# The output stage of a low-rank mixing kernel, by pairs of tiles with seven products

## The chip, the cores and the metric

One core of a Trainium2 chip. The metric is device time in microseconds. A kernel's number is the median of its runs.

## The reference

`x` is 32 sequences of 64 tokens with 1024 features; each sequence has one id of 0 to 7. Cut to what matters:

```python
base   = x @ W.T
logits = x @ Wr.T + 5.0 * one_hot(id)            # 8 experts
gates  = softmax over the two largest logits, 0 elsewhere
h      = einsum('btd,erd->bter', x, A)           # rank 16 for each expert
c      = base + 2.0 * einsum('bter,bte,eor->bto', h, gates, B)
out    = x + c @ (U * S @ V.T).T                 # rank 256
```

The kernel never forms `c`. It computes P = W^T V (1024 x 256) and (B^T V), then for each tile of 128 tokens z = x P + (gated h) (2 B^T V), 128 x 256, and the output z (U S)^T + x.

## The kernel before

All is float32 accuracy made of two reduced parts: each operand is split into `hi` (a cast to fp32r, on ACT) and `lo` (the difference, on DVE or POOL), and `triple` (L243) makes three matmuls of it: hi hi, hi lo, lo hi. There are 16 tiles and five queues that run on their own, held together by semaphores.

- **Start.** W and V arrive in chunks; TensorE makes P in two halves of 8 chunks (`p_chunk`), with ACT and DVE splitting each chunk (`split_w`, `split_v`) in the order i = 0 to 15. P's banks are split into `proj_hi`, `proj_lo`.
- **TensorE, `step(s)`.** `project(s, k)` for 8 values of k (24 matmuls of 392 columns: 128 for h, 8 logits, 256 for z); within it `transpose_gh(s-1)` after k = 1 and `mix(s-1)` after k = 4, which adds the gated part into tile s-1's z; then `transpose_z(s-1)` and the output of tile s-2, `expand(s-2, n)` for two halves of 512 columns, 6 matmuls of 128x512 each. Four banks `fin` are used in turn. Step 2 differs: gh at k = 5, mixing after the last k.
- **DVE, `step(s)`.** `split_gh(s-1)`, `gates_top(s)` (begins at L509 when tile s is projected), `gates_apply(s)` (waits for ACT's exponential), then `residual(s-2, 0)`, `split_z(s-1)`, `residual(s-2, 1)`: bank plus x, into `x_all`.
- **ACT, `step(s)`.** `split_x(s+1)` (xT_hi, L428), the copies `ghT_hi` (L439), `z_sb` (L441), `zT_hi` (L443), then the exponential of tile s (L446). Each waits for its input in that order.
- **POOL.** Only xT_lo (L237) for tiles 0 to 15. TensorE's step s waits for xT_lo of tile s; ACT's xT_hi of tile t waits until tile t-2 is projected.
- **SP.** All loads and stores; the ids (8 KB) after W, then the second tile, S and U. DVE converts them (L593) and compares them (L595) after `b_lo` (L590) and before the gates of tile 0. `us_hi`, `us_lo` (L431, L502) are U times S, of 128x1024 each for m = 0, 1.

After step 15 TensorE still has the outputs of tiles 13, 14 and 15 (36 matmuls' worth of 128x512), with the gh and z of tile 15 between.

## Time and profile before

| | us |
|---|---|
| median of 3 runs (163.03 to 164.63) | 163.12 |
| profiled execution | 163.83 |
| its span, first to last instruction | 161.8 |
| TensorE busy | 156.5 |
| DVE busy | 83.8 |
| ACT busy | 55.4 |
| POOL busy | 40.4 |

Times within the execution are counted from the start of its span. A row of the timeline gives an instruction's start and duration; matmuls overlap, so the engine's pace is read from start to start, not from the duration. What an instruction waited for stands behind it in brackets. The granted clock of TensorE is 1.00 throughout.

### The profile page before, as it was taken

Reading aid. Unit: us, or ns where it says so; the run is one execution under the profiler, and the core shown is the slowest. Engines: PE = TensorE matmul, PEld = TensorE weight load, DVE = VectorE, ACT = ScalarE, POOL = GpSimd, SP = SyncE. Lnnn points to the kernel's source line nnn. Section 1 sums busy time; section 2 is a strip of 40 time slices with the busy share of each in tenths; the row PEclk is TensorE's granted clock in tenths of the full one; section 3 lists DMA queues with packets and bytes.
Section 4 is the critical chain, followed back from the end, with each engine's and each line's share of the span. In section 5 each row is a group of like instructions: output and inputs, shape, how many; then the busy total and the mean of one; then the engine's idle time right before and its main releaser. Section 6 shows DMA issues by size and latency. Waiting matters only on the chain.

```text
span 161.8 us, 2469 instructions
## 1 busy us (share of the span) xinstructions
PE 156.5 (97%) x900; PEld 144.9 (90%) x900; DVE 83.8 (52%) x260; ACT 55.4 (34%) x132; POOL 40.4 (25%) x31
## 2 busy tenths in 40 slices
PE   7899999999899999999999999999999999999992
PEld 4899999999798989898999999898989898989882
DVE  0785785298855271727263535445362627180843
ACT  4765783317334142313223141404141313111210
POOL 2000041070552450505050505050514233200000
DMA  5999999963030659293929393847463430303055
GB/s 176 406 409 400 388 412 408 409 250 130 14 120 0 195 197 297 93 315 110 321 99 302 120 293 124 271 136 253 147 242 134 130 130 0 130 4 130 0 198 191
DMA packets 10522, 32.69 MB, mean 202 GB/s; under 512 B 1424, under 2 KB 1936, under 8 KB 10384
## 3 DMA queue, kind: packets, MB, share of 16 engines
q1 hardware_dynamic: 10224, 31.96, 55.1%
q10 hardware_dynamic: 288, 0.59, 1.0%
q8 instruction: 7, 0.11, 0.3%
q14 instruction: 3, 0.02, 0.0%
HBM read 24.16 MB, written 8.39 MB: 201 GB/s over the span
## 4 chain that ended last, share of the span: by engine, by line
PE 87%; DVE 4%; ACT 3%; DMA 3%; issue 1%; SPq 0%; DVEq 0%
PE fin L244 14%; PE pj L244 14%; PE fin L246 14%; PE fin L245 14%; PE pj L246 14%; PE pj L245 14%; DMA vw_raw<-in_VW 3%; PE zt L303 2%; DVE ids_f L593 1%; PE gt L291 1%; ACT us_hi L431 1%; DVE proj_lo L496 1%; DVE b_lo L590 1%; ACT xT_hi L428 1%; DVE w_lo L487 0%
## 5 line engine op out<-in xcount | busy, mean ns | idle before, releaser
L237 POOL TENSOR_TENSOR xT_lo<-xt_raw,xT_hi 128x1024 fp32r<-128x1024 f32 x16 | 39.3, 2455 | 97.4 <-ACT xT_hi L428 97.4
L244 PE MATMUL pj<-proj_hi,xT_hi 128*128 128x392 f32 x128 | 45.0, 352 | 0.0
L246 PE MATMUL pj<-proj_hi,xT_lo 128*128 128x392 f32 x128 | 43.6, 341 | 0.0
L245 PE MATMUL pj<-proj_lo,xT_hi 128*128 128x392 f32 x128 | 43.4, 339 | 0.0
L244 PE MATMUL fin<-us_hi,zT_hi 128*128 128x512 f32 (+1 forms) x66 | 27.0, 409 | 0.0
L245 PE MATMUL fin<-us_lo,zT_hi 128*128 128x512 f32 (+1 forms) x66 | 25.6, 388 | 0.0
L246 PE MATMUL fin<-us_hi,zT_lo 128*128 128x512 f32 (+1 forms) x66 | 25.6, 388 | 0.0
L244 PEld LDWEIGHTS pj<-proj_hi,xT_hi 128*128 128x128 f32 x128 | 24.0, 188 | 1.1
L245 PEld LDWEIGHTS pj<-proj_lo,xT_hi 128*128 128x128 f32 x128 | 24.1, 188 | 0.6
L246 PEld LDWEIGHTS pj<-proj_hi,xT_lo 128*128 128x128 f32 x128 | 24.0, 188 | 0.0
L509 DVE SCALAR_TENSOR_TENSOR logit<-target,pj 128x8 f32<-128x8 f32 x16 | 2.6, 163 | 39.3 <-PE pj L246 39.3
L554 DVE TENSOR_TENSOR x_all<-fin,x_all 128x512 f32<-128x512 f32 x31 | 21.2, 686 | 2.5 <-PE fin L246 2.5
L244 PE MATMUL fin<-v_hi,w_hi 128*128 128x256 f32 x60 | 17.8, 297 | 0.1
L245 PE MATMUL fin<-v_lo,w_hi 128*128 128x256 f32 x60 | 17.6, 293 | 0.0
L246 PE MATMUL fin<-v_hi,w_lo 128*128 128x256 f32 x60 | 17.5, 292 | 0.0
L428 ACT CAST xT_hi<-xt_raw 128x1024 fp32r<-128x1024 f32 x16 | 16.6, 1039 | 0.0
L246 PEld LDWEIGHTS fin<-us_hi,zT_lo 128*128 128x128 f32 x66 | 12.4, 188 | 2.8
L441 ACT COPY z_sb<-pj 128x256 f32<-128x256 f32 x16 | 6.0, 372 | 25.8 <-PE pj L246 25.8
L439 ACT CAST ghT_hi<-gt 128x128 fp32r<-128x128 f32 x16 | 4.2, 265 | 30.3 <-PE gt L291 30.3
L244 PEld LDWEIGHTS fin<-us_hi,zT_hi 128*128 128x128 f32 x66 | 12.4, 188 | 2.1
L245 PEld LDWEIGHTS fin<-us_lo,zT_hi 128*128 128x128 f32 x66 | 12.5, 189 | 2.0
L443 ACT CAST zT_hi<-zt 128x256 fp32r<-128x256 f32 x16 | 6.0, 374 | 22.2 <-PE zt L303 22.2
(71 smaller groups left out, 195.2 us busy)
## 6 DMA issues: line engine op xcount, KB each, us to landing
xt_raw<-in_xt SPq DMA_DIRECT2D x16, 512.0 KB, 4.2
x_all<-in_x SPq DMA_DIRECT2D x16, 512.0 KB, 3.8
out<-x_all SPq DMA_DIRECT2D x14, 512.0 KB, 2.9
vw_raw<-in_VW SPq DMA_DIRECT2D x6, 384.0 KB, 6.2
w_raw<-in_W SPq DMA_DIRECT2D x8, 256.0 KB, 9.9
u_raw<-in_U SPq DMA_DIRECT2D x1, 1024.0 KB, 12.6
out<-x_all SPq DMA_DIRECT2D x3, 256.0 KB, 2.0
aw_raw<-in_AW SPq DMA_DIRECT2D x1, 544.0 KB, 8.3
```

The costliest lines, as they stand in the source:

```text
L237: nc.gpsimd.tensor_sub(xT_lo[:, t % 2, :, :], xt_raw[:, t % XTR, :, :], xT_hi[:, t % 2, :, :].bitcast(F32)).then_inc(xt_lo, 1)
L244: nc.tensor.matmul(dst, l_hi, r_hi, start=first, stop=False, skip_group_check=shared)
L245: nc.tensor.matmul(dst, l_hi, r_lo, start=False, stop=False, skip_group_check=shared)
L246: return nc.tensor.matmul(dst, l_lo, r_hi, start=False, stop=last, skip_group_check=shared)
L291: nc.tensor.transpose(gt[:, 0:P], gh[:, :], ident[:, :]).then_inc(gt_done, 1)
L303: last = nc.tensor.transpose(zt[:, m * P:(m + 1) * P], z_sb[:, m * P:(m + 1) * P], ident[:, :])
L428: nc.scalar.copy(xT_hi[:, t % 2, :, :], xt_raw[:, t % XTR, :, :]).then_inc(xt_hi, 1)
L439: nc.scalar.copy(ghT_hi[:, :], gt[:, 0:P]).then_inc(gt_hi, 1)
L441: nc.scalar.copy(z_sb[:, :], pj[(s - 1) % 2][:, Z0:COLS]).then_inc(z_copied, 1)
L443: nc.scalar.copy(zT_hi[:, (s - 1) % 2, :], zt[:, 0:RANK]).then_inc(zt_hi, 1)
L509: nc.vector.scalar_tensor_tensor(logit[:, :], target[:, s, :], LANG_BIAS, pj[q][:, LOG:LOG + E], ALU.mult, ALU.add).then_inc(gate_step, 1)
L554: nc.vector.tensor_add(x_all[:, t % XR, cols], fin_bank(i)[:, :], x_all[:, t % XR, cols]).then_inc(fin_free, 1)
```

## The change

The output of two tiles (128 rows each) by two halves of U S (m = 0, 1) and two column halves is a 2 x 2 block product. It is done in Strassen's form (Winograd's variant) with 7 products instead of 8, each a `triple` of 128x512. Sums on the z side (`sums`, four of 128 columns, DVE) and on the U S side (`make_tsum`, four of 128x512, POOL, once) go before, and sums of products after: `copy_u` (ACT), `up` (DVE), `side` (POOL, adds into x_all), and four residuals. Each sum is split into hi and lo anew (`split_zb`, `split_t`). Pairs 0 to 6 go that way, in two parts: five products after an odd step, two after the even step behind it. Tiles 14 and 15 are done plainly as before. A pair's outputs begin after step 2p+3, so after step 15 there are 45 matmuls' worth of 128x512. In step 2 and 3 gh stands at k = 4 and mixing after k = 6. z of an odd tile goes to the other half of bank `zt`. The ids are loaded before W and converted in `make_target` at i = 8 of DVE's splitting order. The core of the diff:

```diff
+            def store_pair(p):
+                sp.wait_ge(fin_read, READS * p + 6)
+                sp.dma_start(out_v[2 * p, :, :], x_all[:, (2 * p) % XR, :]).then_inc(stored[(2 * p) % XR], 16)
+                sp.wait_ge(side_add, ADDS * p + 3)
+                sp.dma_start(out_v[2 * p + 1, :, :], x_all[:, (2 * p + 1) % XR, :]).then_inc(stored[(2 * p + 1) % XR], 16)
...
             load_w(0)
             load_w(1)
             sp.dma_start(aw_raw[:, :, :], AW).then_inc(aw_load, 16)
@@ -195,7 +223,6 @@
...
-            for t in range(TILES):
+
+            def split_x(t):
                 pool.wait_ge(xt_hi, t + 1)
                 nc.gpsimd.tensor_sub(xT_lo[:, t % 2, :, :], xt_raw[:, t % XTR, :, :],
                                      xT_hi[:, t % 2, :, :].bitcast(F32)).then_inc(xt_lo, 1)
+
+            def make_tsum():
+                pool.wait_ge(y_done, 2)
+                nc.gpsimd.tensor_sub(tsum[:, 0, :], y[:, 0, BANK:], y[:, 0, 0:BANK]).then_inc(tsum_done, 1)
+                nc.gpsimd.tensor_sub(tsum[:, 2, :], y[:, 1, BANK:], y[:, 0, BANK:]).then_inc(tsum_done, 1)
+                pool.wait_ge(tsum_done, 1)
+                nc.gpsimd.tensor_sub(tsum[:, 1, :], y[:, 1, BANK:], tsum[:, 0, :]).then_inc(tsum_done, 1)
+                pool.wait_ge(tsum_done, 3)
+                nc.gpsimd.tensor_sub(tsum[:, 3, :], y[:, 1, 0:BANK], tsum[:, 1, :]).then_inc(tsum_done, 1)
+
+            def side(t, n, j):
+                cols = slice(n * BANK, (n + 1) * BANK)
+                pool.wait_ge(x_load[t % XR], 16 * (t // XR + 1))
+                nc.gpsimd.tensor_add(x_all[:, t % XR, cols], x_all[:, t % XR, cols], ups[:, j, :]).then_inc(side_add, 1)
+
+            for t in range(3):
+                split_x(t)
+            make_tsum()
+            split_x(3)
+            split_x(4)
+            for p in range(SP_PAIRS):
+                pool.wait_ge(fin_read, READS * p + 1)
+                side(2 * p + 1, 0, 1)
+                side(2 * p, 1, 1)
+                if 2 * p + 5 < TILES:
+                    split_x(2 * p + 5)
+                pool.wait_ge(fin_read, READS * p + 3)
+                side(2 * p + 1, 1, 2)
+                if 2 * p + 6 < TILES:
+                    split_x(2 * p + 6)
 
 
         @block.tensor
...
             def transpose_z(t):
                 pe.wait_ge(z_copied, t + 1)
-                if t >= 1:
-                    pe.wait_ge(zt_lo, t)
+                if t >= 2 and t % 2 == 0:
+                    pe.wait_ge(za_lo, t // 2)
+                    pe.wait_ge(sums_done, 4 * (t // 2))
+                if t >= 2 and t % 2 == 1:
+                    pe.wait_ge(sums_done, 4 * (t // 2))
+                c = RANK * (t % 2)
                 for m in range(MC):
...
+            def product(p, dst, x, y_hi, y_lo, first, last):
+                q = p % 2
+                triple(dst[:, :], zh[:, q, x, :], zl[:, q, x, :], y_hi, y_lo, first, last, shared=True).then_inc(prod, 1)
+
...
+            def p1(p):
+                pe.wait_ge(za_lo, p + 1)
+                if p >= 1:
+                    pe.wait_ge(fin_read, READS * (p - 1) + 4)
+                product(p, bank_a, 0, *us(0, 0), True, False)
+
+            def p6(p):
+                pe.wait_ge(zb_lo, p + 1)
+                if p >= 1:
+                    pe.wait_ge(fin_read, READS * (p - 1) + 1)
+                product(p, bank_b, 4, *t_of(1), True, True)
+
+            def p7(p):
+                if p >= 1:
+                    pe.wait_ge(fin_read, READS * (p - 1) + 5)
+                product(p, bank_c, 5, *t_of(2), True, False)
+
+            def p5(p):
+                if p >= 1:
+                    pe.wait_ge(fin_read, READS * (p - 1) + 6)
+                product(p, bank_d, 3, *t_of(0), True, False)
+
...
+            def p2(p):
+                pe.wait_ge(u_copied, p + 1)
+                product(p, bank_a, 1, *us(1, 0), False, True)
+
+            def p4(p):
+                pe.wait_ge(fin_read, READS * p + 2)
+                product(p, bank_c, 2, *t_of(3), False, True)
+
+            def p3(p):
+                pe.wait_ge(fin_read, READS * p + 3)
+                product(p, bank_d, 6, *us(1, 1), False, True)
+
+            def first_part(p):
+                if p == 0:
+                    pe.wait_ge(us_lo_done, MC)
+                    pe.wait_ge(tl_done, 2)
+                p1(p)
+                p6(p)
+                p7(p)
+                p5(p)
+                p2(p)
+
+            def second_part(p):
+                p4(p)
+                p3(p)
+
+            def expand_end(dst, x, lo, hi):
+                q = (PAIRS - 1) % 2
                 for m in range(MC):
-                    zk = slice(m * P, (m + 1) * P)
-                    last = triple(fin_bank(i)[:, 0:BANK // 2], zT_hi[:, q, zk], zT_lo[:, q, zk],
-                                  us_hi[:, m, o], us_lo[:, m, o], m == 0, m == MC - 1)
-                last.then_inc(fin_done, 1)
+                    last = triple(dst[:, 0:hi - lo], zh[:, q, x + m, :], zl[:, q, x + m, :],
+                                  us_hi[:, m, lo:hi], us_lo[:, m, lo:hi], m == 0, m == MC - 1)
...
-            def step(s, gh_at=1, mix_at=4, z_after=None):
+            def step(s, gh_at=1, mix_at=4):
                 pe.wait_ge(xt_lo, s + 1)
-                if s >= 2:
...
                         transpose_gh(s - 1)
-                    if s >= 1 and k == mix_at and k < DC - 1:
+                    if s >= 1 and k == mix_at:
                         if s == 1:
                             pe.wait_ge(bv_lo_done, 1)
                         mix(s - 1)
                 last.then_inc(pj_done, 1)
                 if s == 0:
                     make_bv()
-                if s >= 1 and mix_at == DC - 1:
-                    mix(s - 1)
-                if s >= 1 and z_after is None:
+                if s >= 1:
                     transpose_z(s - 1)
-                if s == 2:
-                    pe.wait_ge(us_lo_done, MC)
-                if s >= 2 and s < LAST:
-                    for n in range(HALF):
-                        expand(s - 2, n)
-                        if z_after == n:
-                            transpose_z(s - 1)
+                if s >= 3 and s % 2 == 1 and s < LAST:
...
-            for s in range(3, TILES):
+            step(2, gh_at=4, mix_at=6)
+            step(3, gh_at=4, mix_at=6)
+            for s in range(4, TILES):
                 step(s)
 
-            expand(LAST - 2, 0)
-            expand(LAST - 2, 1, parts=[0])
+            p = SP_PAIRS - 1
+            p1(p)
+            p6(p)
+            p7(p)
+            p5(p)
             transpose_gh(LAST)
-            expand(LAST - 2, 1, parts=[1])
-            expand(LAST - 1, 0, parts=[0])
+            p2(p)
+            p4(p)
             mix(LAST)
-            expand(LAST - 1, 0, parts=[1])
+            p3(p)
             transpose_z(LAST)
-            expand(LAST - 1, 1)
-            expand(LAST, 0)
-            for j in range(2):
-                expand_end(j)
+            pe.wait_ge(za_lo, PAIRS)
+            pe.wait_ge(fin_read, READS * p + 1)
+            expand_end(bank_b, 0, 0, BANK)
+            pe.wait_ge(fin_read, READS * p + 4)
+            expand_end(bank_a, 0, BANK, D)
...
+            def make_y(m):
+                nc.scalar.activation(y[:, m, :], u_raw[:, m, :], ACT.Copy, scale=s_col[:, m:m + 1]).then_inc(y_done, 1)
+
+            def split_t(b):
+                act.wait_ge(tsum_done, 2 * b + 2 if b == 1 else 3)
+                nc.scalar.copy(th[:, 2 * b:2 * b + 2, :], tsum[:, 2 * b:2 * b + 2, :]).then_inc(th_done, 1)
+
+            def split_za(t):
+                p = t // 2
+                act.wait_ge(zt_done, t + 1)
+                if p >= 2:
+                    act.wait_ge(prod, PRODS * (p - 1))
+                nc.scalar.copy(zh[:, p % 2, 0:MC, :], zt[:, 0:RANK].rearrange("p (m n) -> p m n", m=MC)).then_inc(za_hi, 1)
...
+            def split_zb(t):
+                p = t // 2
+                act.wait_ge(zt_done, t + 1)
+                if p >= 1:
+                    act.wait_ge(zb_lo, p)
+                nc.scalar.copy(zs[:, 0, :], zt[:, RANK + P:2 * RANK]).then_inc(x22_copied, 1)
+                act.wait_ge(sums_done, 4 * p + 4)
+                nc.scalar.copy(zh[:, p % 2, 2:7, :], zs[:, :, :]).then_inc(zb_hi, 1)
+
+            def copy_u(p):
+                act.wait_ge(prod, PRODS * p + 1)
+                if p >= 1:
+                    act.wait_ge(fin_read, READS * (p - 1) + 1)
+                nc.scalar.copy(ups[:, 0, :], bank_a[:, :]).then_inc(u_copied, 1)
+
...
+            def exp_top(s):
+                act.wait_ge(dtop_ready, s + 1)
+                nc.scalar.activation(etop[:, :], dtop[:, :], ACT.Exp, accum_out=esum[:, :]).then_inc(exp_done, 1)
+
             def step(s):
-                if s >= 1 and s + 1 < TILES:
+                if s + 1 < TILES:
                     split_x(s + 1)
-                if s >= 1:
-                    act.wait_ge(gt_done, s)
-                    nc.scalar.copy(ghT_hi[:, :], gt[:, 0:P]).then_inc(gt_hi, 1)
-                    act.wait_ge(z_done, s)
-                    nc.scalar.copy(z_sb[:, :], pj[(s - 1) % 2][:, Z0:COLS]).then_inc(z_copied, 1)
-                    act.wait_ge(zt_done, s)
-                    nc.scalar.copy(zT_hi[:, (s - 1) % 2, :], zt[:, 0:RANK]).then_inc(zt_hi, 1)
-                if s < TILES:
-                    act.wait_ge(dtop_ready, s + 1)
-                    nc.scalar.activation(etop[:, :], dtop[:, :], ACT.Exp, accum_out=esum[:, :]).then_inc(exp_done, 1)
+                hand_on(s - 1)
+                if s % 2 == 1:
+                    split_za(s - 1)
+                    exp_top(s)
+                    if s == 1:
+                        for m in range(MC):
+                            make_y(m)
+                    if s >= 3:
+                        copy_u((s - 3) // 2)
+                else:
+                    if s == 2:
+                        for b in range(2):
+                            split_t(b)
+                    exp_top(s)
+                    split_zb(s - 1)
...
+            def make_target():
+                dve.wait_ge(ids_load, 16)
+                dve.wait_ge(const, 3 + E)
+                nc.vector.tensor_copy(ids_f[:, :], ids_i[:, :]).then_inc(setup, 1)
+                dve.wait_ge(setup, 1)
+                nc.vector.tensor_tensor(
...
+            def split_t(b):
+                dve.wait_ge(th_done, b + 1)
+                nc.vector.tensor_sub(tl[:, 2 * b:2 * b + 2, :], tsum[:, 2 * b:2 * b + 2, :],
+                                     th[:, 2 * b:2 * b + 2, :].bitcast(F32)).then_inc(tl_done, 1)
...
+            def sums(p):
+                n = 4 * p
+                dve.wait_ge(x22_copied, p + 1)
+                nc.vector.tensor_add(zs[:, 1, :], zt[:, RANK:RANK + P], zs[:, 0, :]).then_inc(sums_done, 1)
+                dve.wait_ge(sums_done, n + 1)
+                nc.vector.tensor_sub(zs[:, 2, :], zs[:, 1, :], zt[:, 0:P]).then_inc(sums_done, 1)
+                dve.wait_ge(sums_done, n + 2)
+                nc.vector.tensor_sub(zs[:, 3, :], zs[:, 0, :], zs[:, 2, :]).then_inc(sums_done, 1)
+                nc.vector.tensor_sub(zs[:, 4, :], zt[:, P:RANK], zs[:, 2, :]).then_inc(sums_done, 1)
+
+            def split_zb(p):
+                dve.wait_ge(zb_hi, p + 1)
+                nc.vector.tensor_sub(zl[:, p % 2, 2:7, :], zs[:, :, :],
+                                     zh[:, p % 2, 2:7, :].bitcast(F32)).then_inc(zb_lo, 1)
+
+            def up(p, j):
+                if j == 1:
+                    dve.wait_ge(u_copied, p + 1)
+                dve.wait_ge(prod, PRODS * p + j + 1)
+                if p >= 1:
+                    dve.wait_ge(side_add, ADDS * (p - 1) + 1 + j)
+                if j == 2:
+                    dve.wait_ge(fin_read, READS * p + 1)
+                nc.vector.tensor_add(ups[:, j, :], (bank_b if j == 1 else bank_c)[:, :], ups[:, j - 1, :]).then_inc(fin_read, 1)
+
...
+            def xb0(p):
+                dve.wait_ge(side_add, ADDS * p + 1)
+                residual(p, bank_c, 6, 2 * p + 1, 0)
+
...
             def step(s):
-                if s >= 1:
-                    split_gh(s - 1)
+                if s == 3:
+                    for b in range(2):
+                        split_t(b)
+                if s >= 3 and s % 2 == 1:
+                    split_zb((s - 3) // 2)
                 gates_top(s)
                 gates_apply(s)
-                if s >= 2 and s < LAST:
-                    residual(s - 2, 0)
-                if s >= 1:
-                    split_z(s - 1)
-                if s >= 2 and s < LAST:
-                    residual(s - 2, 1)
+                if s % 2 == 1:
+                    if s >= 3 and s < LAST:
+                        p = (s - 3) // 2
+                        up(p, 1)
+                        up(p, 2)
+                        xb1(p)
+                        xa0(p)
+                    if s < LAST:
+                        split_za(s - 1)
+                        split_gh(s)
+                else:
+                    sums((s - 2) // 2)
+                    split_gh(s)
+                    if s >= 4:
+                        p = (s - 4) // 2
+                        xb0(p)
+                        xa1(p)
 
             for i in range(2 * OC):
                 if i < OC:
                     split_v(i)
                 split_w(i)
+                if i == OC:
+                    make_target()
...
+            up(p, 2)
             split_gh(LAST)
-            residual(LAST - 2, 0)
-            residual(LAST - 2, 1)
-            split_z(LAST)
-            residual(LAST - 1, 0)
-            residual(LAST - 1, 1)
-            residual(LAST, 0)
-            for j in range(2):
-                residual_end(j)
+            split_za(LAST - 1)
+            xb1(p)
+            xa0(p)
+            xb0(p)
+            dve.wait_ge(zb_hi, PAIRS)
+            nc.vector.tensor_sub(zl[:, (PAIRS - 1) % 2, MC:2 * MC, :], zt[:, RANK:2 * RANK].rearrange("p (m n) -> p m n", m=MC),
+                                 zh[:, (PAIRS - 1) % 2, MC:2 * MC, :].bitcast(F32)).then_inc(zb_lo, 1)
+            xa1(p)
+            residual_end(0, bank_b, LAST - 1, 0, BANK)
+            residual_end(1, bank_a, LAST - 1, BANK, D)
+            residual_end(2, bank_c, LAST, 0, BANK)
+            residual_end(3, bank_d, LAST, BANK, BANK + BANK // 2)
+            residual_end(4, bank_b, LAST, BANK + BANK // 2, D)
 
```

## Rows read from the trace of the kernel before

**Rows 1.** Busy time by engine, summed over windows of the whole span; count of instructions in brackets.

```profile
sum 162.00, PE 156.52 PEld 144.87 DVE 83.82 ACT 55.40 POOL 40.39; mean PE 9.78 PEld 9.05 DVE 5.24 ACT 3.46 POOL 2.52
```

**Rows 2.** Waits of TensorE: who waited for whom, total us, times, longest.

```profile
PE pj L244 <- DVE ghT_lo L541: 0.8, 1, 0.8
```

**Rows 3.** Timeline of TensorE in one step: start us, duration us, engine, line, instruction.

```profile
87.74 0.40 PE L245 MATMUL fin<-us_lo,zT_hi 128*128 128x512 f32 x1
...
90.31 0.34 PE L244 MATMUL pj<-proj_hi,xT_hi 128*128 128x392 f32 x1
...
91.37 0.27 PE L291 MATMUL gt<-ident,gh 128*128 128x128 f32 x1
...
93.08 0.28 PE L244 MATMUL pj<-bv_hi,ghT_hi 128*128 128x256 f32 x1
```

**Rows 4.** Timelines of DVE, ACT and POOL in the same step.

```profile
87.49 0.16 DVE L509 SCALAR_TENSOR_TENSOR logit<-target,pj 128x8 f32<-128x8 f32 x1 [2.98 <-PE pj L246]
...
89.34 0.68 DVE L554 TENSOR_TENSOR x_all<-fin,x_all 128x512 f32<-128x512 f32 x1
...
91.97 0.29 DVE L541 TENSOR_TENSOR ghT_lo<-gt,ghT_hi 128x128 fp32r<-128x128 f32 x1 [0.78 <-ACT ghT_hi L439]
...
95.25 0.16 DVE L509 SCALAR_TENSOR_TENSOR logit<-target,pj 128x8 f32<-128x8 f32 x1 [2.98 <-PE pj L246]
...
88.27 0.20 ACT L446 ACTIVATE etop<-dtop 128x2 f32<-128x2 f32 x1 [0.19 <-DVE dtop L514]
...
89.59 2.41 POOL L237 TENSOR_TENSOR xT_lo<-xt_raw,xT_hi 128x1024 fp32r<-128x1024 f32 x1 [5.36 <-ACT xT_hi L428]
```

**Rows 5.** Timelines of POOL, DVE, ACT and TensorE around steps 0 and 1.

```profile
32.86 3.19 POOL L237 TENSOR_TENSOR xT_lo<-xt_raw,xT_hi 128x1024 fp32r<-128x1024 f32 x1 [8.02 <-ACT xT_hi L428]
...
40.88 2.38 POOL L237 TENSOR_TENSOR xT_lo<-xt_raw,xT_hi 128x1024 fp32r<-128x1024 f32 x1 [4.83 <-ACT xT_hi L428]
...
33.72 2.36 DVE L593 CAST ids_f<-ids_i 128x16 f32<-128x16 int32 x1
...
41.20 3.13 DVE L502 SCALAR_TENSOR_TENSOR us_lo<-u_raw,s_col,us_hi 128x1024 fp32r<-128x1024 f32 x1
...
38.47 0.36 ACT L477 ACTIVATE bv_hi<-zt 128x256 fp32r<-128x256 f32 x1
...
39.77 1.03 ACT L428 CAST xT_hi<-xt_raw 128x1024 fp32r<-128x1024 f32 x1
...
40.70 0.26 ACT L439 CAST ghT_hi<-gt 128x128 fp32r<-128x128 f32 x1
...
37.61 0.29 PE L246 MATMUL zt<-v_hi,b_lo 128*128 128x256 f32 x1
...
41.44 0.36 PE L244 MATMUL pj<-bv_hi,ghT_hi 128*128 128x256 f32 x1 [0.76 <-DVE ghT_lo L541]
```

**Rows 6.** Timelines of SP and DVE in the start.

```profile
10.08 1.10 SPq L198 DMA_DIRECT2D ids_i<-in_ids  x1
...
17.07 0.69 DVE L487 TENSOR_TENSOR w_lo<-w_raw,w_hi 128x512 fp32r<-128x512 f32 x1 [0.75 <-ACT w_hi L413]
```

**Rows 7.** Groups of instructions by form: busy us, mean ns of one, idle before and releaser.

```profile
L413 ACT CAST w_hi<-w_raw 128x512 fp32r<-128x512 f32 x8 | 5.0, 622 | 3.2 <-PE fin L246 3.2
...
L460 ACT CAST proj_hi<-aw_raw 128x1088 fp32r<-128x1088 f32 x1 | 1.1, 1101 | 0.0
...
L431 ACT ACTIVATE us_hi<-u_raw,s_col 128x1024 fp32r<-128x1024 f32 x2 | 2.3, 1140 | 0.0
...
L590 DVE TENSOR_TENSOR b_lo<-b_raw,b_hi 128x1024 fp32r<-128x1024 f32 x1 | 1.2, 1215 | 0.0
...
L554 DVE TENSOR_TENSOR x_all<-fin,x_all 128x512 f32<-128x512 f32 x31 | 21.2, 686 | 2.5 <-PE fin L246 2.5
...
L246 PE MATMUL fin<-us_hi,zT_lo 128*128 128x512 f32 x62 | 24.5, 395 | 0.0
...
L374 PE MATMUL fin<-zeros 128*128 128x512 f32 x6 | 2.9, 656 | 1.0 <-POOL zeros L228 1.0
```

More of the change, by code:

```diff
@@ L197, in _ @@
                 load_w(k)
-            sp.dma_start(ids_i[:, :], ids).then_inc(ids_load, 16)
             load_xt(1)
@@ L294, in mix @@
                 pe.wait_ge(gt_lo, t + 1)
-                triple(pj[t % 2][:, Z0:COLS], ghT_hi[:, :], ghT_lo[:, :], bv_hi[:, :], bv_lo[:, :],
+                triple(pj_bank(t)[:, Z0:COLS], ghT_hi[:, :], ghT_lo[:, :], bv_hi[:, :], bv_lo[:, :],
                        False, True, shared=True).then_inc(z_done, 1)
@@ L332, in make_bv @@
+                last.then_inc(end_prod, 1)
             def make_bv():
@@ L471, in _ @@
             split_x(1)
-            step(0)
+            exp_top(0)
             act.wait_ge(s_load, 16)
@@ L478, in _ @@
             scale_u(1)
-            for s in range(1, TILES + 1):
+            for s in range(1, TILES):
                 step(s)
+            hand_on(LAST)
+            act.wait_ge(zt_done, LAST + 1)
+            nc.scalar.copy(zh[:, (PAIRS - 1) % 2, MC:2 * MC, :],
+                           zt[:, RANK:2 * RANK].rearrange("p (m n) -> p m n", m=MC)).then_inc(zb_hi, 1)
         @block.vector
```

178 lines of the change are left out of this document (100 added, 78 removed).

## The prediction

> **What bounds the kernel now.** I read the page's busy shares first, then the waits, then the timelines of one step, engine by engine. [rows 1] sums them: TensorE 156.5 us of a span of 161.8, DVE 83.8, ACT 55.4, POOL 40.4, so only TensorE is full. [rows 2] is the one wait of TensorE behind another engine after the first few microseconds, 0.8 us before one mixing matmul. So in the loop matmul time is the time. In [rows 3] one step runs from 87.49 (the first gate instruction, L509; I call this moment L, and count from it) to 95.25, 7.76 us. The twelve 128x512 matmuls start 0.2334 us apart (87.74 to 90.31 is eleven of them). The next tile's projection starts at L+2.82, the transpose of gh at L+3.88, the mixing matmuls at L+5.59, and the next L is 4.94 after the projection's start. [rows 4] shows how much room the other engines have: DVE finishes the gates at L+1.85 (89.34) and has ghT_lo at L+4.77, so the mixing matmul finds its operand 0.8 us early. That room is what the change spends.
>
> **What it removes.** Seven pairs go from 24 to 21 matmuls of 128x512: 21 x 0.2334 = 4.90 us off TensorE. The last pair keeps its 24. Bytes moved stay the same.
>
> **The ids.** The cast at L593 took 2.36 us for 16 columns [rows 5]. It ended at 36.08, when POOL's xT_lo ended (32.86 + 3.19 = 36.05). us_lo (L502) in the same group, 3.13 us beside POOL's 40.88 to 43.26, has its own 1.07 us behind POOL's end; and POOL's 3.19 instead of 2.38 began under DVE's b_lo. I read it as exclusive use: where a DVE instruction with both inputs in SBUF meets a POOL one, the later waits out the earlier. Moving the cast to i = 8 puts it where DVE idles (0.75 us before 17.07 [rows 6]) and POOL has nothing. Its DMA (1.10 us of SP's queue) now stands ahead of W's, but nobody waits for W: ACT's idle before its copies of it ends with TensorE, not with a DMA [rows 7]. The gates of tile 0 come 1.3 us earlier, but the path goes over ACT: bv_hi can't start before the last B^T V matmul ends (37.61 + 0.29), 0.5 us earlier than its 38.47 [rows 5]. Then us_hi, xT_hi, ghT_hi and ghT_lo follow as before, and mix(0) starts at 40.98, not 41.44: -0.46 us.
>
> **Step 2.** ACT now does make_y (two 128x1024 scalings of 1.14 us, as us_hi [rows 7]) after the exponential of tile 1 and before xT_hi(3) and ghT_hi(1). us_lo still waits for POOL's xT_lo(2) (now to 42.8) and ends at 44.1; the gates follow; exp comes 0.78 after their first [rows 4], at 44.8, and make_y runs to 47.2, each ACT instruction starting 0.09 or 0.10 before the end of the one ahead where nothing holds it (39.77 + 1.03 against 40.70 in [rows 5]), xT_hi(3) to 48.15, ghT_hi to 48.33, ghT_lo to 48.65, mix(1) at 48.80. TensorE would be there at 47.35, with projection 2 begun at 43.24, the mixing after seven of its eight k (3 matmuls of 0.178 each; eight of them with the extras make the 4.94 of a step) and no output matmuls before it: 1.45 us lost. The transpose of gh at k = 4 waits 0.20 for gh, and that of z, one k behind the mixing, 0.18 for z_sb.
>
> **Step 3.** POOL does make_tsum before split_x(3). It waits for y (47.2). Its four 128x512 subtractions have no row. POOL's 128x1024 takes 2.41 [rows 4]; half of it is 1.21. From below 1.0 (if the rate were better on f32 output), from above 1.4 (half, and a fixed part of 0.2, which is what ACT's 512 and 1088 columns leave when their slope is taken off [rows 7]); I take 1.21, the same elements at the same rate. So 47.28 + 4 x 1.21 + 0.2 (one wait behind a DVE gate instruction) = 52.3, then xT_lo(3) to 54.7. TensorE, which has no output matmul in step 2, is ready at 50.2: projection 3 starts at 54.8, 4.60 us lost. POOL standing idle before did not show that its queue can be the path.
>
> The Trainium skill (GPSIMD Engine Reference, section Performance versus the Vector engine) gives 4497 ns for a 2048-element add on GpSimd; halved twice that is 1.12 us, an estimate, and the sum would be 0.4 us smaller. No row here has that size.
>
> **First pair.** Everything for the products is ready but tl, t's low part. ACT's first th copy waits for tsum, and exp(2) stands behind both th copies (to 53.3), then the gates, whose two-input instructions also wait for xT_lo(3) (54.7), sums(0) to 56.5, the copy of the five parts, xT_hi(4) to 58.2, ghT_hi(2) and ghT_lo(2) to 58.7. mix(2) loses 0.11, z's transpose 0.18. DVE has split_t behind that, two instructions of 1.22 (as b_lo, L590 in [rows 7]) with both inputs in SBUF, and POOL has started xT_lo(4) at 58.3: DVE gets in at 60.7 and is through at 63.1. TensorE stands since 60.3: 2.92 us. zb_lo of pair 0 (640 columns, 0.82) is there 0.2 us before P6 asks.
>
> **Each later pair.** After an even step only 6 output matmuls (1.40 us) separate the projections, so the next projection starts at L+1.42, gh's transpose L+2.48, mixing L+4.19. DVE: gates to L+1.85; sums, four of 128 columns (0.29 each, as ghT_lo), the first three chained: 0.33 + 0.33 + 0.21 + 0.29 = 1.16, to L+3.01. Then ACT, which stands at that wait with xT_hi and ghT_hi of the next tile behind it: the 640-column copy. 512 columns take 0.62 and 1088 take 1.10 [rows 7], so 0.73, between 0.62 and 1.04 at the outside; its successor starts 0.09 before its end: L+3.68. xT_hi 0.95: L+4.63. ghT_hi 0.27, ghT_lo 0.29, each with 0.03 of signalling: L+5.21; 0.15 to TensorE: L+5.35. Against 4.19 that is 1.16 us lost at mix(4), (6), (8), (10) and (12). mix(14) has no xT_hi ahead of it: 0.21. The odd steps, with 15 matmuls between, hide all they have: gh's transpose at L+4.57, u's copy, two ups and two residuals of 0.69 (L554 in [rows 7]) end at L+4.9, ghT_lo at about L+5.2, mixing at L+6.28. POOL there: three side additions (1.21) and two xT_lo, 8.5 us of 16, behind nobody on TensorE's path; without that cover each microsecond of it would come back 7 times.
>
> If the later-waits-for-earlier rule held only for long instructions, the gates of tile 2 would not wait for POOL and the sum were 1.1 us smaller. The Trainium skill (SBUF — State Buffer, Who interferes with whom) makes it a matter of two SBUF inputs against a GpSimd instruction that reads SBUF, whatever the length: by that 11.4, by long ones alone 10.3. [rows 5] agrees for 128x1024; no row here has a short one beside POOL.
>
> **Tail.** 45 matmul-equivalents instead of 36 are in the terms above already. P3 waits 0.11 for the read of its bank. The last stores follow the last additions as before.
>
> **Sum.** Waits: 0.20 + 1.45 + 0.18 + 4.60 + 0.11 + 0.18 + 2.92 + 5 x 1.16 + 0.21 + 0.11 = 15.76. After a wait the first matmul holds the engine about 0.07 longer (0.36 in [rows 5], 0.28 in [rows 3]): 14 x 0.07 = 0.98. 15.76 + 0.98 - 4.90 - 0.46 = +11.4 us. The profiled execution took 163.83 (span 161.8), so 175.2 for its like; the median of the runs is 163.12, which gives 174.5.
>
> **Rivals.**
> - *DVE and POOL do not exclude each other* (the two long rows would have another cause). Then mix(1) loses 0.91, tl 0.78, mix(2) nothing: +8.2, 171.3 us. Against it: three ends in [rows 5] match. 10%.
> - *The steady waits vanish*: ACT's chain would have to be 1.16 us shorter, which even a free 640-column copy does not give. Only the start is paid: 11.4 - 6.4 = +5.0, 168.1. For it, every piece is small and its overlap estimated; 4%.
> - *TensorE's clock falls in the 4.6 us it stands*: the zero matmuls of the start, after idling, took 0.656 each [rows 7] against 0.395 in the loop. The row of a loop matmul is in the same group. Step 3's projection (4.3 us) at half speed adds up to 4.3, of which 2.9 lie in the wait for tl: +1.4 to +1.8, 176 us. The granted clock is 1.00 everywhere in this trace, which speaks against. 15%.
> - *Faster: TensorE stays the bound*. Place: its queue. All products' savings arrive if the added waits stay under 5.4 us, the point from which it decides; with none, 163.12 - 4.90 - 0.46 = 157.8. In its favour stands [rows 1] alone; against it, each of two places by itself (the wait for xT_lo(3), the mixes) nearly reaches that sum, with durations that have rows. 4%.
> - Forecast, 174.5, own range 172 to 176.7 (POOL's size 1.0 gives -0.7, 1.4 gives +2.1; ACT's copy at 0.9 +1.2; short instructions free -1.1): 67%.
>
> Range 169 to 178. About 1% is what a measurement of this kernel tells from no change; slower by more than that in all but the fast rival: 0.94; same 0.02, faster 0.04.
>
> **What would show it.** Waits list: TensorE behind xT_lo once for 4 to 5 us, behind tl_lo about 3, behind ghT_lo six or seven times, five at 1.1 to 1.2. Steps after the start: pairs 16.05 us instead of 15.53. 21 fewer matmuls of 128x512; ids_f under 0.3 us. Wrong would be: no ghT_lo waits (the ACT order is harmless), POOL's 128x512 far from 1.2, or the pair at 14.8.

## The result, and the profile after

The changed kernel takes 173.3 us (median, 172.41 to 175.77), the kernel before 163.07 in the same comparison: ratio 1.060, 95% interval 1.055 to 1.066. It is 10.2 us slower. The ratio goes by the faster three of its four runs, since the fourth, 175.77, lies over 1.5% above the fastest. The profiled execution took 173.07 with a span of 171.3, against 163.83 and 161.8. Forecast were 174.5 us and, for the span, +11.4; measured were 173.3 and +9.5.

The page of the changed kernel, its span and part 1 (busy time, share, instructions), which answer to [rows 1], and the line of the granted clock in 40 slices:

```profile
span 171.3 us, 2562 instructions
PE 154.6 (90%) x879; PEld 141.4 (83%) x879; DVE 107.8 (63%) x304; ACT 65.9 (38%) x150; POOL 71.4 (42%) x56
PEclk9999999999985899999999999999999999999999
```

TensorE executes 21 matmuls fewer and is busy 1.9 us less, not 4.9. Of the 3.0 us between, 1.5 are nine matmuls at a lower clock (slices 12 to 14, below). Another 1.3 belong to the five steady waits: a wait is counted from the modelled end of the matmul before it, so that 0.26 us of each still counts as busy (a pair of steps is busy for 15.02 us, and takes 14.76 where it has no wait). Its idle time went from 5.3 us to 16.7. The waits say behind whom (columns: who waited, for whom, total us, times, longest); [rows 2] had one line, of 0.8:

```profile
PE pj L301 <- DVE ghT_lo L706: 5.9, 7, 1.2
PE pj L301 <- POOL xT_lo L264: 4.5, 1, 4.5
PE fin L301 <- issue: 1.3, 1, 1.3
```

The first is the mixing matmul, whose operand is late for tiles 0, 1, 4, 6, 8, 10 and 12; the second is the projection of tile 3, once; the third turns out to be the first product, which waits for t's low part. In this kernel's traces the small parts have the names of the buffers that they reuse: v_hi and v_lo are the two parts of t, the sums on the U S side; w_hi and w_lo are those of z and its sums; vw_raw holds y (U times S, for the sums), tsum and u. TensorE's timeline at these places (start, duration, operation, and in brackets the idle time ahead, counted from the modelled end of the matmul before):

```profile
40.28 0.36 PE L301 MATMUL pj<-bv_hi,ghT_hi 128*128 128x256 f32 x1 [0.24 <-DVE ghT_lo L706]
47.73 0.39 PE L301 MATMUL pj<-bv_hi,ghT_hi 128*128 128x256 f32 x1 [1.16 <-DVE ghT_lo L706]
53.77 0.69 PE L301 MATMUL pj<-proj_hi,xT_hi 128*128 128x392 f32 x1 [4.52 <-POOL xT_lo L264]
54.26 0.53 PE L302 MATMUL pj<-proj_lo,xT_hi 128*128 128x392 f32 x1
54.58 0.53 PE L303 MATMUL pj<-proj_hi,xT_lo 128*128 128x392 f32 x1
...
61.87 0.47 PE L301 MATMUL fin<-us_hi,w_hi 128*128 128x512 f32 x1 [1.26 <-issue]
...
91.58 0.39 PE L301 MATMUL pj<-bv_hi,ghT_hi 128*128 128x256 f32 x1 [0.88 <-DVE ghT_lo L706]
107.48 0.39 PE L301 MATMUL pj<-bv_hi,ghT_hi 128*128 128x256 f32 x1 [0.88 <-DVE ghT_lo L706]
```

Two steady mixes are 15.90 us apart, where a pair took 15.53 before. Behind the wait of 4.5 us the matmuls last 0.53 us and start 0.33 apart, against 0.34 and 0.178 elsewhere: the lower of the two clocks.

Why projection 3 waits, from POOL's timeline (same columns): the sums for tsum (two of the four stand here) wait for ACT's y and go ahead of tile 3's low part. Why the first product waits, from DVE's last row: the two halves of t's low part stand behind ghT_lo(2) and have to wait until POOL is through with tile 4 (59.55).

```profile
46.34 1.27 POOL L269 TENSOR_TENSOR vw_raw<-vw_raw 128x512 f32<-128x512 f32 x1 [4.22 <-ACT vw_raw L543]
50.14 1.27 POOL L274 TENSOR_TENSOR vw_raw<-vw_raw 128x512 f32<-128x512 f32 x1
51.37 2.34 POOL L264 TENSOR_TENSOR xT_lo<-xt_raw,xT_hi 128x1024 fp32r<-128x1024 f32 x1
57.16 2.39 POOL L264 TENSOR_TENSOR xT_lo<-xt_raw,xT_hi 128x1024 fp32r<-128x1024 f32 x1 [3.45 <-ACT xT_hi L536]
58.81 2.96 DVE L710 TENSOR_TENSOR v_lo<-vw_raw,v_hi 128x1024 fp32r<-128x1024 f32 x2
```

Why every even mix waits, from the timelines of DVE, ACT and TensorE at tile 4 (its first gate instruction, the L of the prediction, is at 70.34). In the step of [rows 3], with L at 87.49, ACT copied the next xT_hi at L+0.98, and ghT_hi at L+4.19 as soon as TensorE had the transpose:

```profile
88.47 1.04 ACT L428 CAST xT_hi<-xt_raw 128x1024 fp32r<-128x1024 f32 x1
91.68 0.27 ACT L439 CAST ghT_hi<-gt 128x128 fp32r<-128x128 f32 x1 [2.17 <-PE gt L291]
```

In the changed kernel it stands 1.79 us for DVE's sums with both copies behind it, which come at L+3.75 and L+4.70:

```profile
70.34 0.16 DVE L675 SCALAR_TENSOR_TENSOR logit<-target,pj 128x8 f32<-128x8 f32 x1 [2.88 <-PE pj L303]
73.46 0.73 ACT L563 CAST w_hi<-zs 128x640 fp32r<-128x640 f32 x1 [1.79 <-DVE zs L727]
74.09 1.04 ACT L536 CAST xT_hi<-xt_raw 128x1024 fp32r<-128x1024 f32 x1
75.04 0.26 ACT L573 CAST ghT_hi<-gt 128x128 fp32r<-128x128 f32 x1
75.33 0.29 DVE L706 TENSOR_TENSOR ghT_lo<-gt,ghT_hi 128x128 fp32r<-128x128 f32 x1 [1.90 <-ACT ghT_hi L573]
75.67 0.39 PE L301 MATMUL pj<-bv_hi,ghT_hi 128*128 128x256 f32 x1 [0.98 <-DVE ghT_lo L706]
```

### The profile page after: what moved, and what is told of

Same layout as the page of the kernel before. It is cut to its first block, busy times and chain, and to the rows that moved or that the text cites. A ratio compares the mean times of both kernels' runs of the same rounds, so it can differ in the third digit from the quotient of the medians.

```text
span 171.3 us, 2562 instructions
## 1 busy us (share of the span) xinstructions
PE 154.6 (90%) x879; PEld 141.4 (83%) x879; DVE 107.8 (63%) x304; ACT 65.9 (38%) x150; POOL 71.4 (42%) x56
## 4 chain that ended last, share of the span: by engine, by line
PE 70%; DVE 11%; ACT 7%; POOL 4%; issue 4%; DMA 2%; DVEq 0%; ACTq 0%
PE pj L301 11%; PE fin L301 11%; PE fin L303 11%; PE fin L302 11%; PE pj L303 10%; PE pj L302 10%; ACT xT_hi L536 4%; DVE us_lo L658 2%; DMA vw_raw<-in_VW 2%; POOL xT_lo L264 1%; PE zt L364 1%; ACT vw_raw L543 1%; DVE ghT_lo L706 1%; DVE gh L699 1%; DVE zs L724 1%
## 5 line engine op out<-in xcount | busy, mean ns | idle before, releaser
L279 POOL TENSOR_TENSOR x_all<-x_all,vw_raw 128x512 f32<-128x512 f32 x21 | 26.8, 1292 | 30.0 <-DVE vw_raw L742 30.0
L301 PE MATMUL fin<-v_hi,w_hi 128*128 128x256 f32 (+1 forms) x88 | 29.0, 330 | 0.0
L302 PE MATMUL fin<-v_lo,w_hi 128*128 128x256 f32 (+1 forms) x88 | 28.2, 321 | 0.0
L303 PE MATMUL fin<-v_hi,w_lo 128*128 128x256 f32 (+1 forms) x88 | 28.2, 321 | 0.0
L301 PEld LDWEIGHTS fin<-v_hi,w_hi 128*128 128x128 f32 x88 | 17.2, 195 | 1.3 <-DVE w_lo L643 0.2
L303 PEld LDWEIGHTS fin<-v_hi,w_lo 128*128 128x128 f32 x88 | 17.1, 194 | 1.2
L302 PEld LDWEIGHTS fin<-v_lo,w_hi 128*128 128x128 f32 x88 | 17.2, 195 | 0.9
L536 ACT CAST xT_hi<-xt_raw 128x1024 fp32r<-128x1024 f32 x16 | 16.7, 1046 | 0.0
L301 PE MATMUL fin<-us_hi,w_hi 128*128 128x512 f32 (+1 forms) x31 | 12.6, 405 | 1.3 <-issue 1.3
L303 PE MATMUL fin<-us_hi,w_lo 128*128 128x512 f32 (+1 forms) x31 | 11.7, 378 | 0.0
L302 PE MATMUL fin<-us_lo,w_hi 128*128 128x512 f32 (+1 forms) x31 | 11.7, 378 | 0.0
```

The lines of the kernel that those rows point to most:

```text
L279: nc.gpsimd.tensor_add(x_all[:, t % XR, cols], x_all[:, t % XR, cols], ups[:, j, :]).then_inc(side_add, 1)
L301: nc.tensor.matmul(dst, l_hi, r_hi, start=first, stop=False, skip_group_check=shared)
L302: nc.tensor.matmul(dst, l_hi, r_lo, start=False, stop=False, skip_group_check=shared)
L303: return nc.tensor.matmul(dst, l_lo, r_hi, start=False, stop=last, skip_group_check=shared)
L536: nc.scalar.copy(xT_hi[:, t % 2, :, :], xt_raw[:, t % XTR, :, :]).then_inc(xt_hi, 1)
```

## Experiments

The theory: the products save what was said, and two places in two queues cost more, ACT's order in the odd steps and the place of tsum in the queues at the start.

**1. The steady wait.** ACT copies ghT_hi ahead of the five parts of the odd step (and so ahead of xT_hi too); nothing else is changed. In outline:

```diff
+                if first_gh:            # s >= 3 and odd
+                    copy_gh(s - 1)      # ghT_hi
+                    copy_zb((s - 3) // 2)   # waits for sums, copies 640 columns
                 if s + 1 < TILES:
                     split_x(s + 1)
```

> Edit: on ACT the next tile's ghT_hi copy stands before the 640-column copy of the five sums and before xT_hi; nothing else moves. Theory (ACT's queue costs the even tiles' mixing about 0.9 us each, five times, and part of the wait for tl): the waits of TensorE behind ghT_lo at tiles 4 to 12 vanish, a pair takes 14.9 us instead of 15.9, and the median falls by 5 to 7.7 us, to 165.6 to 168.3. Rival (the exclusion between DVE and POOL, not ACT's order, holds the pairs up): the waits stay or come back as waits of P6 for zb_lo, a pair stays above 15.6 and the median above 171.

Measured: 170.35 us, ratio 1.045 (1.035 to 1.055); 2.95 us less than the changed kernel. The waits of the even mixes are gone, and two steps take 14.76 us (logits at 94.68 and 109.44), so the theory of the wait holds. 5 x (15.90 - 14.76) = 5.7 us should have come back, and only 2.95 did: the expectation of 5 to 7.7 was too high. The rest was lost in the first pair. There one sign of the rival came, P6 waiting for the low part of the z side; its others, a pair above 15.6 us and a median above 171, did not. DVE, POOL and TensorE of this kernel there:

```profile
60.29 3.15 POOL L264 TENSOR_TENSOR xT_lo<-xt_raw,xT_hi 128x1024 fp32r<-128x1024 f32 x1 [7.49 <-ACT xT_hi L536]
61.14 2.98 DVE L742 TENSOR_TENSOR w_lo<-zs,w_hi 128x640 fp32r<-128x640 f32 x1
64.18 0.50 PE L301 MATMUL fin<-v_hi,w_hi 128*128 128x512 f32 x1 [1.92 <-DVE w_lo L742]
```

The low part of the five z parts (w_lo in the trace), 0.82 us by itself, takes 2.98 because POOL's xT_lo had begun 0.85 us ahead of it; POOL itself, which began under another DVE instruction, takes 3.15 for 2.41. P6, the first matmul that needs it, waits 1.92 us. From 65.67 on nine matmuls run at the low clock (starts 0.43 us apart for 512 columns and 0.33 for 392).

**2. The place of tsum.** POOL does all four xT_lo first:

```diff
-            for t in range(3):
+            for t in range(4):
                 split_x(t)
             make_tsum()
-            split_x(3)
```

> Edit: POOL makes xT_lo of tile 3 before its four subtractions for the U S sums, not after. Theory (the chain from the subtractions goes on over ACT's th copies, exp(2) and gh(2), so that POOL's order alone moves the wait): the 4.5 us wait before projection 3 shrinks to about 0.5, but a wait of 4 us or more appears within step 3 at the transpose of gh, and the median rises by 1 to 3 us, to 174.3 to 176.3. Rival (POOL's queue alone is the cause): the median falls by about 4 us, to 169.

Measured: 177.41 us (177.26 to 177.47), ratio 1.088; 4.1 more than the changed kernel. The wait for xT_lo(3) falls to 0.43, and the lateness comes back a few instructions on, larger: gh's transpose waits 4.23 us, the mixing 1.20 and the first product 1.81. The place was as expected, the rise (1 to 3 us) was expected too small. From TensorE's and ACT's timelines:

```profile
49.98 0.45 PE L300 MATMUL pj<-proj_hi,xT_hi 128*128 128x392 f32 x1 [0.43 <-POOL xT_lo L264]
57.17 0.33 PE L347 MATMUL gt<-ident,gh 128*128 128x128 f32 x1 [4.23 <-DVE gh L698]
53.67 1.04 ACT L546 CAST v_hi<-vw_raw 128x1024 fp32r<-128x1024 f32 x1 [4.61 <-POOL vw_raw L272]
55.96 0.20 ACT L578 ACTIVATE etop<-dtop 128x2 f32<-128x2 f32 x1
```

tsum now comes later, ACT's copy of it stands at the head of ACT's queue in step 2, and exp(2), the gates and gh(2) wait behind that. It isn't POOL's order by itself that costs, but that a chain (y by ACT, tsum by POOL, th by ACT, tl by DVE) runs through three queues whose next entries TensorE needs.

**3. The chain earlier.** make_y goes ahead of ACT's last two copies of P (proj_hi), for which it waited 5.05 us in the changed kernel; tsum goes right behind xT_lo(0), and the th copies into step 1. POOL's part of the edit:

```diff
-            for t in range(3):
-                split_x(t)
+            split_x(0)
             make_tsum()
-            split_x(3)
+            for t in range(1, 4):
+                split_x(t)
```

> Edit: U S scaled for the sums (make_y) on ACT before P's last split, where it idles, POOL's four subtractions right after the first tile's xT_lo, the two th copies on ACT in step 1 behind z_sb. Theory (once the sums are made early, steps 2 and 3 run as the projection allows): the 4.5 us wait before projection 3 and the 1.2 us one at mix(1) are gone, the wait for tl stays at 1 to 3 us, the pairs stay at 15.9 us; the median falls by 4.5 to 6 us, to 167.3 to 168.8. Rival (the early POOL work blocks DVE's b_lo and us_lo and ACT's start): the gain is below 2 us.

Measured: 170.24 us, ratio 1.044 (1.036 to 1.052); 3.06 less, where 4.5 to 6 were expected. The 4.5 us and the wait of mix(1) are gone. But DVE still makes tl in step 3, now under POOL's xT_lo(4): its two instructions of 1.22 us take 4.26. The first product waits 2.69 us for it instead of 1.26, and seven matmuls from there run at the low clock; mix(2) waits 0.97, mix(0) 0.55. The pairs stay at 15.9.

```profile
52.36 2.37 POOL L264 TENSOR_TENSOR xT_lo<-xt_raw,xT_hi 128x1024 fp32r<-128x1024 f32 x1 [4.69 <-ACT xT_hi L536]
52.68 4.26 DVE L709 TENSOR_TENSOR v_lo<-vw_raw,v_hi 128x1024 fp32r<-128x1024 f32 x2
```

**4. Both, 1 and 3 together.**

> Edit: both the early sums and the ghT_hi copy ahead. Theory (both places are independent and the saved 21 matmuls then count in full): a pair at 14.9 us, start waits about 1.5 us in all, median 159 to 161.5, faster than the kernel before at 163.1. Rival (with the pairs tighter another resource binds, DVE with POOL): gain less than the sum of the two alone by over 2 us, median above 163.

Measured: 162.76 us, ratio 0.995 (0.991 to 0.9996); 10.5 us less than the changed kernel and level with the kernel before, where 159 to 161.5 was expected. The account against the changed kernel, from the traces: the first product starts at 54.16 instead of 61.87 (7.7 us), five pairs at 14.70 instead of 15.90 (6.0), less what the first pair now loses, P6 at 57.01 where 54.92 was possible (2.1) and eight steps that take 0.425 on average where 0.23 is full pace (1.6): 10.0, and the spans differ by 10.4. DVE, POOL and TensorE at that loss, and the window (us, busy time of PE, PEld, DVE, ACT and POOL, granted clock, DMA share, GB/s):

```profile
53.11 3.16 POOL L264 TENSOR_TENSOR xT_lo<-xt_raw,xT_hi 128x1024 fp32r<-128x1024 f32 x1 [5.05 <-ACT xT_hi L536]
53.97 2.98 DVE L741 TENSOR_TENSOR w_lo<-zs,w_hi 128x640 fp32r<-128x640 f32 x1
57.01 0.80 PE L301 MATMUL fin<-v_hi,w_hi 128*128 128x512 f32 x1 [1.93 <-DVE w_lo L741]
56.00:60.00 4.00, 2.99 (x7) 2.41 (x8) 3.18 (x13) 1.71 (x4) 0.74 (x2) 0.59 0.38 131
```

The two edits bring 3 us each alone and 10.5 together, because alone each leaves a loss in the first pair that eats about half of it. In experiment 1 that loss is P6, 2.1 us late behind w_lo, and the low clock, 1.6. In experiment 3 it is mix(2), 0.97, the first product, 2.69 where 0.35 is left in experiment 4, and the low clock, 1.4. Together only the 2.1 and 1.6 of the account are paid: with ghT_hi copied first, DVE gets to tl at 51.70, ahead of POOL's xT_lo(4) at 53.11, and w_lo alone is shut out.

**5. Is it the exclusion?** Experiment 4, and POOL begins xT_lo(4) only when that low part is made (`pool.wait_ge(zb_lo, 1)` ahead of `split_x(4)`): POOL works later, and if the exclusion is the cause, TensorE gains.

> Edit on e4_both: POOL starts xT_lo of tile 4 only when the first pair's zb_lo is done. Theory (DVE and POOL exclude each other: there zb_lo took 2.98 us instead of 0.8 since POOL's xT_lo came between, P6 waited 1.93 us and TensorE ran 3.5 us at half speed after it): zb_lo takes 0.8 us, the wait of P6 falls below 0.3 us, the matmuls behind it keep 0.23 us from start to start, and the median falls by 3 to 3.8 us, to 159 to 159.8. Rival (the slow stretch and the length of zb_lo have another cause): zb_lo stays long, the median within 0.5 us of e4_both.

Measured: 160.66 us (160.51 to 160.77), ratio 0.986 (0.983 to 0.989), granted clock 1.00 (0.999 in one execution). The low part takes 0.82, P6 doesn't wait, and the next DVE instruction takes the blow:

```profile
53.59 0.82 DVE L742 TENSOR_TENSOR w_lo<-zs,w_hi 128x640 fp32r<-128x640 f32 x1
54.48 2.40 POOL L264 TENSOR_TENSOR xT_lo<-xt_raw,xT_hi 128x1024 fp32r<-128x1024 f32 x1 [6.81 <-DVE w_lo L742]
54.83 2.07 DVE L691 TENSOR_SCALAR dtop<-top 128x2 f32<-128x2 f32 x1
57.76 0.50 PE L302 MATMUL fin<-us_hi,w_hi 128*128 128x512 f32 x1 [0.97 <-ACT vw_raw L572]
```

dtop, 0.23 us where POOL stands (its row is in experiment 9), takes 2.07 and ends as POOL ends (56.90 and 56.88). Behind it stand exp on ACT, then ACT's copy of u, for which TensorE's fifth product, P2, waits 0.97. The median was expected at 159 to 159.8, so that wait is about what it was short by.

**6. Is the half speed from standing?** Experiment 4 again with eight matmuls of zeros, 128x512, in the gap between P1 and P6 of the first pair, into a bank that a product overwrites later; DVE and POOL do what they did.

> Edit on e4_both: eight 128x512 matmuls of zeros into bank d, which the next product overwrites, stand between P1 and P6 of the first pair, 1.87 us of work where TensorE waits 1.93 us. Nothing waits less. Theory (the half speed behind the wait comes from TensorE's own standing): the stretch at half speed is gone and the median falls by 1.5 to 2 us against e4_both, to 160.8 to 161.3. Rival (the slow stretch comes with the products' operands or banks): the products behind P6 still start 0.43 us apart, no gain.

```profile
54.46 2.00 PE L309 MATMUL fin<-zeros 128*128 128x512 f32 x8
56.58 0.50 PE L301 MATMUL fin<-v_hi,w_hi 128*128 128x512 f32 x1
56.91 0.40 PE L302 MATMUL fin<-v_lo,w_hi 128*128 128x512 f32 x1
```

Measured: 161.21 us (161.01 to 161.73), 1.55 less than experiment 4, as large as the 1.6 of the account there. With TensorE kept at work the products run at full pace, so in the traced execution 1.93 us of standing cost 1.6 us more. It isn't so in every execution: of the ten of experiment 4, the two with a mean granted clock of 1.00 and 0.995 took 161.25 and 161.4 us, as the filled kernel does, and the other eight, at 0.978 to 0.989, took 162.5 to 164.3. No trace of those two was kept.

**7. The same filling in the changed kernel**, 17 matmuls of zeros ahead of step 3, into a bank overwritten later:

> The changed kernel with seventeen 128x512 matmuls of zeros into bank a (overwritten by P1) ahead of step 3, 3.97 us of work inside the 4.5 us wait for xT_lo. Theory (the half speed behind that wait is covered: the t sums' low part can't start before POOL ends xT_lo of tile 4, whatever TensorE does): the first nine matmuls of projection 3 return to 0.178 us apart, which is 1.3 us, the wait ahead of P1 grows by about as much, and the median stays within 0.5 us of 173.3. Rival (the clock's fall is on the path): the median falls by 1.3 us or more.

```profile
48.47 4.14 PE L309 MATMUL fin<-zeros 128*128 128x512 f32 x17
53.33 0.44 PE L301 MATMUL pj<-proj_hi,xT_hi 128*128 128x392 f32 x1 [0.72 <-POOL xT_lo L264]
61.41 0.48 PE L301 MATMUL fin<-us_hi,w_hi 128*128 128x512 f32 x1 [2.71 <-issue]
```

Measured: 173.9 us, ratio 1.065 (1.061 to 1.069), against 173.3 and 1.060: no gain, though 0.1 us outside the 0.5 that was expected. Projection 3 ran at full pace, and the wait for tl grew from 1.26 to 2.71, so the low clock there had been covered by that wait: the first product starts 21.66 us after mix(0) (39.75), in the changed kernel 21.59 after it. The low clock came after the longer wait instead (starts 0.43 apart from 62.97 to 65.96).

**8. The ids alone**, in the kernel before:

```diff
+            sp.dma_start(ids_i[:, :], ids).then_inc(ids_load, 16)   # ahead of load_w(0)
+                if i == OC:
+                    nc.vector.tensor_copy(ids_f[:, :], ids_i[:, :]).then_inc(setup, 1)
```

> The kernel before with one part of the change alone: the ids loaded before W, and converted in DVE's splitting order. Theory: the cast takes under 0.3 us, and mix(0) starts 0.46 us earlier, since ACT's bv_hi is held by the last B^T V matmul: median 0.3 to 0.6 us below the kernel before. Rival (the whole length of the cast was on the path): 1.3 to 2.3 us less; or none at all.

Measured: 162.89 us beside 163.18, ratio 0.999 (0.997 to 1.001): by time alone not told from nothing. The trace shows the step. The cast takes 0.17 us, and mix(0) starts 1.01 us earlier than in [rows 5] (40.43 against 41.44):

```profile
37.44 0.39 ACT L477 ACTIVATE bv_hi<-zt 128x256 fp32r<-128x256 f32 x1 [0.49 <-PE zt L246]
40.43 0.36 PE L244 MATMUL pj<-bv_hi,ghT_hi 128*128 128x256 f32 x1 [0.25 <-DVE ghT_lo L541]
```

Half of that isn't the edit's. In this execution and in that of the changed kernel TensorE reached full pace earlier in its first microseconds, and the last B^T V matmul came at 37.1 and 36.97 instead of 37.61. Wait by wait, 0.76 to 0.25, the edit is worth 0.5 us; the medians differ by 0.29, within the noise.

**9 and 10. What is left of the first pair.** In experiment 9, on top of 4, POOL waits until DVE has made dtop of tile 3 (`pool.wait_ge(dtop_ready, 4)`), and so passes both the low part and dtop.

> Edit on e4_both: POOL starts xT_lo of tile 4 only when DVE has made dtop of tile 3 (in e6 it started ahead of it, and dtop, a one-input tensor_scalar of two columns, took 2.07 us instead of 0.23). Theory (dtop too is shut out by POOL, and exp, u's copy and P2 hang on it): dtop takes 0.23 us, the 0.97 us wait of P2 behind u's copy in e6 is gone, a new wait for xT_lo before projection 4 is 0.2 to 0.5 us; median 159.8 to 160.3, that is 0.4 to 0.8 below e6. Rival (dtop's length had another cause): no change against e6 or worse.

```profile
55.02 0.23 DVE L691 TENSOR_SCALAR dtop<-top 128x2 f32<-128x2 f32 x1
55.42 2.34 DVE L694 TENSOR_TENSOR chosen<-iota_e,top_i 128x16 f32<-128x16 f32 x1
61.74 0.39 PE L302 MATMUL pj<-bv_hi,ghT_hi 128*128 128x256 f32 x1 [0.89 <-DVE ghT_lo L717]
```

Measured: 160.94 us (160.85 to 161.1), where 159.8 to 160.3 was expected, and not less than the 160.66 of experiment 5 (ratio 0.986 to the kernel before in both). The wait for u is gone, and the exclusion falls on chosen, two instructions on; gh(3) and mix(3) are late by 0.89 instead. Experiment 10 adds that DVE makes the first half of tl in step 2, after the sums, and only the second in step 3:

```diff
                 if s == 3:
-                    for b in range(2):
-                        split_t(b)
+                    split_t(1)
...
                     sums((s - 2) // 2)
+                    if s == 2:
+                        split_t(0)
```

> Edit on e10: on DVE the first half of the t sums' low part is made ahead of ghT_lo of tile 2 instead of behind it. Theory: mix(2) waits 0.4 to 0.6 us more for ghT_lo, and the first pair 1.2 us less for tl and zb_lo, of which only 0.35 us was a wait; median within 0.4 us of e10. Rival (the first pair's chain over DVE still binds): 0.5 us or more less than e10.

Measured: 160.21 us (160.03 to 161.91), ratio 0.983 (0.977 to 0.989), 0.73 less than experiment 9. Expected was no more than 0.4 of difference; the rival, that the first pair's chain over DVE still bound, said 0.5 or more and held. This is the best of the versions, 1.7% below the kernel before. The first product starts at 53.34 instead of 53.95 and its wait is gone, while mix(2) comes only 0.18 later (52.06 for 51.88). The wait of mix(3), 0.89, is not gone.

## Why the prediction was right, and where it was not

- **The saved matmuls.** As said, 21 fewer. They show in full only with the queues mended: two steps took 15.53 before and 14.70 to 14.76 in experiments 1 and 4, where 15.53 - 3 x 0.2334 gives 14.83. The products run slightly closer together (nine starts from 63.36 to 65.40, 0.227 apart).
- **Steady waits, 5 x 1.16.** Right, the mechanism and the size. Measured, each pair loses 15.90 - 14.76 = 1.14 with the slower start of the first matmul in it; predicted were 1.16 + 0.07. The chain that the text built from pieces, mixing at L+5.35, came at 75.67 - 70.34 = L+5.33. Experiment 1 removed the wait by the order of ACT's queue alone. The rival without steady waits (168.1) is out.
- **Projection 3, 4.60.** Right: 4.52 in the timeline. POOL's 128x512 took 1.27 to 1.30, inside the bounds of 1.0 and 1.4 and above the 1.21 taken; the four, with starts overlapping a little, took 5.07 us (46.34 to 51.41) for the 5.04 of the sum.
- **The other terms before it.** mix(1) lost 1.16 and not 1.45, with y 0.3 us earlier than the sum had it. The small ones (0.20, 0.18, 0.11 and 0.18 in the first steps, 0.21 and 0.11 at the end) show as no wait of TensorE in the list; they were put too high, by up to 1.0 us in all.
- **tl, 2.92.** 1.26 in the changed kernel, the largest miss among the terms. Experiment 7 shows why: the rival "TensorE's clock falls" took place inside it. It was given 15%, because the granted clock was 1.00 throughout in the kernel before; it fell (0.85 from 41 to 54 us, 0.81 from 54 to 62, rows below), nine matmuls lasted 3.10 us instead of 1.60, and TensorE arrived 1.4 us later at a wait that had to last until 61.8 anyway. With the filling, the wait was 2.71. The rival's price of +1.4 to +1.8 assumed that all of projection 3 would be slow; nine of its 24 matmuls were, and what they lost was covered. The forecast had no such loss in its sum; that these 1.5 us fell just ahead of a wait long enough for them was its luck.

```profile
41.00:54.00 13.00, 7.32 (x42) 6.43 (x41) 7.85 (x23) 6.94 (x14) 8.41 (x6) 0.85 0.11 41
54.00:62.00 8.00, 6.74 (x31) 6.24 (x32) 4.71 (x9) 2.69 (x5) 2.39 (x1) 0.81 0.37 120
```

- **Exclusion of DVE and POOL.** Right, and the rival without it (10%) is out: w_lo 2.98 beside POOL and 0.82 after it was moved. The open question, whether short instructions wait too, is settled. Rows of the changed kernel, from DVE, beside POOL's 50.14 and 51.37 above (0.17 and 0.15 alone):

```profile
50.26 1.18 DVE L683 TENSOR_TENSOR chosen<-iota_e,top_i 128x16 f32<-128x16 f32 x1
52.80 0.94 DVE L693 TENSOR_TENSOR pick<-chosen,etop 128x16 f32<-128x16 f32 x1
```

  Not every short one is shut out: the reciprocal between them (one column, one input) took its usual 0.16 at 52.72, under the same POOL instruction as pick.

  The Trainium skill (SBUF — State Buffer, Who interferes with whom) names no length for the exclusion, and both rows agree with that. For dtop, which has one tensor input, its condition is a mode of two ports that tensor_scalar can enter; the 2.07 us of experiment 5 agree, though no run here shows the mode. Two readings of the prediction were off here. It said that no row had a short instruction beside POOL, but its own row of the ids' cast, 16 columns in 2.36 us, is one. And it put the rule as one on DVE instructions with both inputs in SBUF, which that cast, with one input, doesn't fit, nor dtop: so the rule was too narrow, and experiment 5 moved POOL onto dtop.
- **The ids.** Predicted -0.46 at mix(0). The wait there went from 0.76 to 0.24 (0.52), and to 0.25 in experiment 8.
- **The 1.9 us between +11.4 and +9.5.** Going by moments: mix(0) came at 40.28 and not 40.98, projection 3 at 53.77 and not 54.8, the first product at 61.87 and not 63.2. Of these 1.3 us, 0.64 are TensorE's earlier full pace in its first microseconds, which is no part of the change, and some 0.3 are y, ready at 46.3 and not 47.2, beyond that; the rest, 0.4, would be the small terms before the first product. Five pairs of 15.90 for 16.05 give 0.7 more, which makes 2.0 for the 1.9 to be explained. By medians, where the chance start averages out, the rise was 10.2.

The range of 169 to 178 held the time, the forecast's own range too. The fast rival needed added waits below 5.4 us. TensorE's idle time rose by 11.4 (5.3 to 16.7). In experiment 4 it stays under the 5.4 (160.9 - 152.4 = 8.5, 3.2 more than before), where the low clock still takes up part of the saving; with POOL's start moved as well (experiment 5, 158.7 - 151.8 = 6.9, 1.6 more than before) the kernel is below the one before.
